# A graph network on one Trainium2 core: the begin of an edge pass, the read of its words and the evict of its sort moved

## The reference

```
h = x @ Wn + bn                                   # block 0, four layers of attention
for l in range(4):
    Q, K, V = h @ WQ[l] + bQ[l], h @ WK[l] + bK[l], h @ WV[l] + bV[l]
    scores = sum(Q[dst] * K[src]) * scale
    attn = softmax of scores over the edges of one dst
    h = layernorm(h + segment_sum(attn * V[src], dst) @ WO[l] + bO[l])
x = x + h @ Wout + bout
# block 1: attention of 8 heads with two types of edges
# block 2: weighted mean of the neighbours, concatenated, @ W
# block 3: segment_sum(norm * x[col], row) @ W.T + b
```

## Time and profile before

| | us |
|---|---|
| median of 3 runs | 7103.49 (7101.05 to 7110.28) |
| the profiled execution's own time | 7094.96 |
| its span | 7093.5 |
| mean granted TensorE clock, share of full | 0.811 |
| busy: PE, DVE | 4693.2 (66%), 4300.3 (61%) |
| busy: ACT, POOL | 2623.5 (37%), 4669.2 (66%) |
| POOL's gathers of the four passes (L1973), busy, idle before them | 2307.4, 887.5 |
| the weighing of their rows (L2141), busy | 729.4 |
| DVE's masks of dense units (L2254), busy, idle before them | 289.2, 413.0 |

### The profile page before, as it was taken

The page is one execution under the profiler, slowest core; times in us unless marked ns, Lnnn a source line. Parts: engine busy times, 40 slices in busy tenths (PEclk is TensorE's granted clock), DMA queues, the critical chain, the costliest instruction groups (busy, mean ns, idle before and its releaser), DMA issues. The chain is left out here.

```text
span 7093.5 us, 128253 instructions
## 1 busy us (share of the span) xinstructions
PE 4693.2 (66%) x28386; PEld 3840.8 (54%) x28387; DVE 4300.3 (61%) x13524; ACT 2623.5 (37%) x7476; POOL 4669.2 (66%) x4886
## 2 busy tenths in 40 slices
PE   5420377775777775777667777445555555998999
PEld 4310266654565554665546655323333334997998
DVE  7550266663666654666556666447776765776665
ACT  0200244434444443444444443315555543554111
POOL 1367577774777765777667777337777755776777
PEclk9555688887888887888778888677777776998999
DMA  5310233332333313333233333123333324333332
GB/s 188 99 37 0 62 92 91 88 84 63 87 90 89 89 50 96 89 90 89 62 86 89 89 90 82 49 89 105 105 105 105 105 69 117 97 96 84 96 95 82
DMA packets 404728, 615.56 MB, mean 87 GB/s; under 512 B 213510, under 2 KB 256049, under 8 KB 403940
## 3 DMA queue, kind: packets, MB, share of 16 engines
q0 software_dynamic: 169952, 363.29, 19.0%
q1 hardware_dynamic: 211190, 200.20, 9.9%
q10 hardware_dynamic: 23122, 47.29, 2.0%
HBM read 528.33 MB, written 82.09 MB: 86 GB/s over the span
## 5 line engine op out<-in xcount | busy, mean ns | idle before, releaser
L1973 POOL DMA_INDIRECT rows<-table_d,meta x2432 | 2307.4, 949 | 887.5 <-issue 728.6
L2037 PE MATMUL ps_total<-weighted_rows,ident 128*128 128x129 f32 (+1 forms) x6464 | 1404.3, 374 | 596.8 <-ACT weighted_rows L2197 483.7
L2037 PEld LDWEIGHTS ps_total<-weighted_rows,ident 128*128 128x128 f32 x6464 | 1149.8, 226 | 857.0 <-issue 670.4
L2373 DVE SCALAR_TENSOR_TENSOR prod<-rows,q_rows 128x129 f32<-128x129 f32 x2432 | 690.0, 293 | 639.3 <-issue 391.1
L1973 POOL DMA_INDIRECT rows<-pairs_d,meta x800 | 773.7, 967 | 257.7 <-issue 243.4
L2073 PE MATMUL dense_sums<-x_rows,dense_power_t 128*128 128x129 f32 x3528 | 593.9, 320 | 460.8 <-DVE dense_rows L2264 443.2
L2073 PEld LDWEIGHTS dense_sums<-x_rows,dense_power_t 128*128 128x128 f32 x3528 | 534.0, 230 | 501.5 <-issue 501.5
L2141 ACT ACTIVATE weighted_rows<-rows,power 128x129 f32<-128x129 f32 x2432 | 729.4, 389 | 5.1
L2159 ACT COPY dense_power_t<-dense_turned 128x512 f32<-128x512 f32 x504 | 265.1, 526 | 1030.7 <-PE dense_turned L2064 1022.1
L2197 ACT ACTIVATE weighted_rows<-once_weighted,of_relation 128x136 f32<-128x136 f32 x1600 | 485.6, 393 | 193.6 <-DVE once_weighted L2433 190.3
L2254 DVE CUSTOM_DVE_ANT_0 dense_masked<-dense_scores,dense_masked,dense_least 128x896 f32<-128x896 f32 x252 | 289.2, 1148 | 413.0 <-PE dense_scores L2055 289.9
(11 more groups left out here) (704 smaller groups left out, 8908.3 us busy)
## 6 DMA issues: line engine op xcount, KB each, us to landing
dense_masked<-dense_masks_d SPq DMA_DIRECT2D x252, 448.0 KB
rows<-table_d,meta POOLq DMA_INDIRECT x2432, 2.5
dense_masks_d<-unmasked ACTq DMA_DIRECT2D x9, 3136.0 KB
src_store<-near_window_d SPq DMA_DIRECT2D x50, 384.0 KB, 3.8
near_window<-near_window_d SPq DMA_DIRECT2D x48, 384.0 KB, 3.6
rows<-pairs_d,meta POOLq DMA_INDIRECT x800, 2.8
tile_rows<-table_d,tile_halves POOLq DMA_INDIRECT x441, 2.6
tile_rows<-made_d,tile_halves POOLq DMA_INDIRECT x441, 2.6
```

Of the source, the lines that this page charges most:

```text
L1973: pool.indirect_dma_start(rows[q][:, j, 0:width], None, table_d, bass.IndirectOffsetOnAxis(meta[q][:, j, number:number + 1], 0)).then_inc( ...
L2037: mm = pe.matmul(total[:, q, ds(part, 1), 0:W].rearrange("p a w -> p (a w)"), k.ident[:], wide[:, j % WS, :], start=False, stop=True, skip ...
L2373: own(dve.scalar_tensor_tensor(prod[:, j % 2, :], rows[q][:, j, :], -1.0, query, ALU.mult, ALU.mult, accum_out=score[:, j, :]))
```

## The change

1. *Begin.* The constants are no longer in a block of their own, so the engines don't meet behind them. ACT waits until the first group's list has landed, then issues x as 8 and 41 tiles. `fetch_layer` goes to SP, behind all its turns. PE turns the first two groups of x, turns the queries, scores the first unit, and then turns the other 11 groups, through two other banks; ACT copies the first two groups, the queries, then the other 11.
2. *Words.* PE reads a group's words for q=0 behind the first unit of a part (units 0 and 4), before behind units 2 and 6, and so raises `read[0]` there. The wait for `sum_taken` and the clearing of the sum stay with the adding of the columns.
3. *Sort.* The wait for `placed` and `scattered` and the evict move from step 5, behind the twelfth column of q=0 (j=11), to the head of step 0, behind the second column (j=1). `placed` is no longer waited for in step 2.

```
-        with nc.Block() as block:
-            @block.vector
-            def _(dve):
...
+        constants_of_pass(nc.vector)
...
                     turns(sp, body)
+                    if fetch is not None:
+                        fetch_layer(sp, m, k, *fetch)
...
                         pe.sem_inc(read[q], 1)
-
+                        return loaded
+
+                    def clear_sums(i, q):
                         pe.wait_ge(m["sum_taken"], i * 2 + (q + 1))
                         clear(q)
-                        return loaded
 
                     def add_columns(i, q, loaded, columns):
+                        if columns[0] == 0:
+                            clear_sums(i, q)
...
                                 if u in (0, 4):
                                     count_earlier(i)
+                                    loaded = load_words(i, 0)
                                 if u == 2:
-                                    add_columns(i, 0, load_words(i, 0), range(S))
+                                    add_columns(i, 0, loaded, range(S))
                                 if u == UNITS - 1:
-                                    loaded = load_words(i, 0)
                                     add_columns(i, 0, loaded, range(S // 2))
...
-                        for n in range(XGROUPS):
-                            if n == 0 or n == 6:
-                                pe.wait_ge(m[f"x_loaded{n // 6}"], 16)
-                            if n >= 2:
-                                pe.wait_ge(m["xt"], n - 1)
+                        def turn_x(n):
...
+                        pe.wait_ge(m["x_loaded0"], 16)
+                        turn_x(0)
+                        turn_x(1)
+                        pe.wait_ge(m["xt"], 2)
                         turn_queries(0)
                         scores(0, 0)
+                        pe.wait_ge(m["x_loaded1"], 16)
+                        for n in range(2, XGROUPS):
+                            pe.wait_ge(m["xt"], n - 1)
+                            turn_x(n)
+                        pe.wait_ge(m["xt"], XGROUPS)
                     turns(pe, body)
...
-                        for h, (t0, t1) in enumerate(((0, 24), (24, T))):
+                        act.wait_ge(listed[0], 48)
+                        for h, (t0, t1) in enumerate(((0, XFIRST), (XFIRST, T))):
...
-                    if fetch is not None:
-                        fetch_layer(act, m, k, *fetch)
...
                         if step == 0:
+                            dve.wait_ge(m["placed"], i + 1)
+                            dve.wait_ge(m["scattered"], i * 16 + 16)
+                            own(dve.tensor_copy(so.stretch[:], placed_ps))
+                            own(dve.scalar_tensor_tensor(so.idx[:], so.base[:], float(REGION - SW), so.start[:], ALU.min, ALU.add))
+                            own(dve.tensor_tensor(so.most[:], so.most[:], count_ps, ALU.max))
+                            own.wait()
+                            own(dve.scalar_tensor_tensor(so.base[:], count_ps, so.base[:], so.floor[:, ds(turn, 1)], ALU.add, ALU.max))
+                            dve.sem_inc(m["evicted"], 1)
...
                         if step == 2:
                             own.wait()
-                            dve.wait_ge(m["placed"], i + 1)
...
                         if step == 5:
...
-                            dve.wait_ge(m["scattered"], i * 16 + 16)
-                            own(dve.tensor_copy(so.stretch[:], placed_ps))
...
+XFIRST = 8
```

More of the change, by code:

```diff
@@ L1864, in edge_pass, with x_ps @@
             loaded_masks = [m["mask0"], m["mask1"]]
+            def x_ps(n):
+                return dense_ps[:, n] if n < 2 else (sum_ps, power_ps)[n % 2]
             masks_of = k.masks_d[0:DSPARE].rearrange("(t p c) r -> t p (c r)", p=P, c=NPAD)
@@ L1895, in step_of, with constants_of_pass @@
             return (loaded[j // PAIRS] >> ((6 if j < PAIRS else 0) + 2 * (j % PAIRS))) & 3
-        with nc.Block() as block:
-            @block.vector
-            def _(dve):
[L1900 to L1911, removed]
-                for q in range(2):
[L1913 to L1916, removed]
+        def constants_of_pass(dve):
+            if mode == "heads":
+                for r in range(2):
+                    dve.memset(relation[:, r:r + 1], float(1 - r))
+            if mode == "attend":
+                for q in range(2):
+                    dve.memset(rows[q][:, :, P:P + 1], 1.0)
+                dve.memset(k.x1[:, :, P:P + 1], 1.0)
+                dve.memset(least[:, 0:1], BIG)
+            if sort is not None:
+                dve.tensor_scalar(tile_no, k.iota_t[:], 1.0, None, ALU.add)
+                dve.tensor_copy(slot_no, so.slot_no[:])
+                dve.tensor_copy(keep, so.keep[:].rearrange("p t c -> p (t c)"))
+            for q in range(2):
+                dve.memset(resets[q][:, 0:1], HALF)
+                dve.memset(resets[q][:, S + 1:S + 2], HALF)
+                dve.memset(neg[q][:, :, S + 1:S + 2], HALF)
+            dve.memset(neg[0][:, :, 0:1], HALF)
+        constants_of_pass(nc.vector)
         with nc.Fori(0, epochs) as e:
@@ L2318, in sort_step @@
                             own(dve.tensor_tensor(at[:], before_ps.unsqueeze(2).to_broadcast([P, T, SC]), seen[:], ALU.add))
-                            dve.wait_ge(m["scattered"], i * 16 + 16)
-                            own(dve.tensor_copy(so.stretch[:], placed_ps))
-                            own(dve.scalar_tensor_tensor(so.idx[:], so.base[:], float(REGION - SW), so.start[:], ALU.min, ALU.add))
-                            own(dve.tensor_tensor(so.most[:], so.most[:], count_ps, ALU.max))
-                            own.wait()
-                            own(dve.scalar_tensor_tensor(so.base[:], count_ps, so.base[:], so.floor[:, ds(turn, 1)], ALU.add, ALU.max))
-                            dve.sem_inc(m["evicted"], 1)
                         if step == 6:
@@ L2698, in group_tiles, with fetch_layer @@
     return range(g * GB, min(g * GB + GB, T))
-def fetch_layer(act, m, k, I, l, last):
+def fetch_layer(sp, m, k, I, l, last):
     def matrix(n, j):
@@ L2707, in column @@
         return I[f"L0_gnn_{n}"][ds(j, 1)].rearrange("a (p n) -> (a p) n", n=1)
-    act.dma_start(k.raw["WV"][:], matrix("WV", l)).then_inc(m["fetched"], 16)
-    act.dma_start(k.raw["WO"][:], matrix("WO", l)).then_inc(m["fetched"], 16)
-    act.dma_start(k.bv[:], column("bV", l), allow_slow_non_contiguous=True).then_inc(m["fetched"], 16)
+    sp.dma_start(k.raw["WV"][:], matrix("WV", l)).then_inc(m["fetched"], 16)
+    sp.dma_start(k.raw["WO"][:], matrix("WO", l)).then_inc(m["fetched"], 16)
+    sp.dma_start(k.bv[:], column("bV", l), allow_slow_non_contiguous=True).then_inc(m["fetched"], 16)
     for n, o in (("ln_g", k.gb), ("ln_b", k.bb)):
-        act.dma_start(o[:], I[f"L0_gnn_{n}"][ds(l, 1)].rearrange("a n -> (a n)").partition_broadcast(P)).then_inc(m["fetched"], 16)
+        sp.dma_start(o[:], I[f"L0_gnn_{n}"][ds(l, 1)].rearrange("a n -> (a n)").partition_broadcast(P)).then_inc(m["fetched"], 16)
     if last:
-        act.dma_start(k.w1[:], I["L0_gnn_Wout"]).then_inc(m["fetched"], 16)
-        act.dma_start(k.b1[:], row(I["L0_gnn_bout"])).then_inc(m["fetched"], 16)
+        sp.dma_start(k.w1[:], I["L0_gnn_Wout"]).then_inc(m["fetched"], 16)
+        sp.dma_start(k.b1[:], row(I["L0_gnn_bout"])).then_inc(m["fetched"], 16)
         return
-    act.dma_start(k.raw["WQ"][:], matrix("WQ", l + 1)).then_inc(m["fetched"], 16)
-    act.dma_start(k.raw["WK"][:], matrix("WK", l + 1)).then_inc(m["fetched"], 16)
-    act.dma_start(k.bq[:], column("bQ", l + 1), allow_slow_non_contiguous=True).then_inc(m["fetched"], 16)
-    act.dma_start(k.bk[:], column("bK", l + 1), allow_slow_non_contiguous=True).then_inc(m["fetched"], 16)
+    sp.dma_start(k.raw["WQ"][:], matrix("WQ", l + 1)).then_inc(m["fetched"], 16)
+    sp.dma_start(k.raw["WK"][:], matrix("WK", l + 1)).then_inc(m["fetched"], 16)
+    sp.dma_start(k.bq[:], column("bQ", l + 1), allow_slow_non_contiguous=True).then_inc(m["fetched"], 16)
+    sp.dma_start(k.bk[:], column("bK", l + 1), allow_slow_non_contiguous=True).then_inc(m["fetched"], 16)
 def layer_turn(nc, k, I, l, last):
```

8 lines of the change are left out of this document (4 added, 4 removed).

## The result

The changed kernel takes **6993.68 us** (median of 4, 6990.34 to 6995.27) beside 7103.39 of the kernel before (median of 4, 7101.05 to 7110.28): ratio 0.9844, 95% interval 0.983 to 0.9858, or 110 us less. The forecast was 7021 with a range of 6978 to 7056. Direction and range hold; the gain is a third larger than the forecast 82.

A forecast was written before the change was run, and what follows sets the result against it. POOL's row gathers were taken to bound the middle of a pass. Begin 10.3, loop 5.4 and end 4.6 make 20.3 us a pass, 81 over four, plus 1 for the "heads" pass: 7103.5-82=7021 us, range 6978 to 7056.

The forecast's parts named there:

- Begin, 10.3 us a pass: Start of a pass: second dense unit at 818.6 in place of 828.91, 10.3 us won; bounds 7.4 and 15.7.
- Evict, 0.6 us a pair: Loop: the evict, moved ahead of PE's first score, costs DVE's chain 0.6 us per pair of turns.
- Lists, 10.8 us in the loop: Loop: lists 11.7 us earlier end DVE's 10.8 us of row waits; less nine pairs at 0.6, 5.4 us won.
- Words, "0": Loop: PE's two 302 ns reads move to after the first unit; 0.6 us shifts within a turn, net 0.
- The end, 4.6: End of a pass: POOL no longer late, last group starts behind the weighing; 4.6 us won, bounds 4.6 and 4.9.
- x late: Rival, begin: x bounds and lands at 815.3, so the begin wins only 4.0 us; 7047 us, chance 0.15.
- Lists late: Rival, loop: masks' waits in SP's in-order queue keep lists late, loop gains nothing; 7043 us, chance 0.10.
- POOL the only bound: Rival, loop: DVE keeps up, all 22.4 us of POOL's list waits count; 6954 us, chance 0.05.
- The wait for `placed`: Rival, loop: DVE's step 0 waits 5.0 us for PE's placing in each of 36 pairs; 7201 us, chance 0.05.
- The rule of the Trainium skill: Begin: moving DMAs to another engine saves only sequencer time, usually small; if so, near 7047 us.

The follow-up runs named there:

- evict_mixed: Changed kernel with the evict at the twelfth column in part 0 only; 10208 us, ratio 1.0242, on the slow chip.
- loads_doubled: Changed kernel plus two reads of a constant word on PE at the old place; 10538 us, ratio 1.0569, on the slow chip.
- no_evict: Changed kernel with the evict back at the twelfth column; 6989.84 us, ratio 0.9839, on the first chip.

## Why the prediction was right, and where it fell short

- **Begin, 10.3 us a pass: right in sum, in part by luck.** 9.7 in the trace; by itself, 42 us for four passes, where 10.3x4 is 41. But the 10.3 were worked out for the second dense unit of the first pass, and there the list took 8.3 us, not 5.1 (gathers from 793.87 and not 790.9), the last x landed at 810.7, not 809.0, and the unit came 7.6 us earlier (821.33), not 10.3. The first weighings of the four passes come 7.6, 12.2, 11.6 and 7.1 us earlier; the prediction had read no row of the middle two. By itself the new begin gives 7.0 in the begin and 3.1 in the loop. Which of its parts (no block, x behind the list and split 8 and 41, the weights on SP, the first scores ahead) gives how much was not separated.
- **Evict, 0.6 us a pair: right in size and place, wrong in what it is worth.** In the whole change it costs the loop 3.8 us a pass, 0.5 a pair, but most of that is given back at the begin and the end. By itself it costs 9 us, 0.25 a pair.
- **Lists, 10.8 us in the loop before the evict is taken off: right in mechanism, too large.** DVE's waits for rows went from 10.8 to none, and the release at the old place brings 10.2 back; but that lengthens the loop by 6.1 us a pass and the end by 3.7, 39 us in the whole time. The prediction took a wait that goes for time that is won.
- **Words, "0": the step that failed.** The prediction weighed the two reads of 302 ns as work that PE sheds in one place and takes up in another. It did not ask what else PE's sequencer had to do there: the register work for the 16 columns, which in the old place started only behind the reads. With lists at 6.1, the begin's 3.1 and the evict's 3.8 taken off, 7.4 of the loop's 12.8 us a pass are left for it, 30 us in all; the remainder by the totals is 33. That the total came within the range owes something to these errors' being of either sign.
- **The end, 4.6: near in size (5.4), wrong in the reason.** POOL is late there as before, only less. In the first pass the weighing ends at 1545.35+4.80=1550.15 and the gather that needs it starts at 1552.88, 2.7 us later and straight behind POOL's own work, where it was 4.9; forecast was 0.3. The mean of the four passes is 2.3 us, before 5.1, so 2.8 us a pass are won so. The rest of the 5.4 holds the ninth pair's share of the loop's gain, 12.8/8=1.6; the other 1.0 was not traced.

```profile
1545.35 4.80 ACT L2153 ACTIVATE weighted_rows<-rows,power 128x129 f32<-128x129 f32 x16
```

```profile
1552.88 0.94 POOL L1979 DMA_INDIRECT rows<-table_d,meta  x1 [0.30 <-issue]
```

- **Rivals.** x late: it landed 1.7 us later than forecast, not 6.3. Lists late: no, 9.3 us earlier. POOL the only bound: no, it now waits 7.8 us for weighed rows, and DVE's circle with PE stands. The wait for `placed`: DVE is never idle before any of the 72 evicts in the trace of the changed kernel. The rule of the Trainium skill, "DMA: Bandwidth & Descriptors", section "Issuing engines are not separate DMA queues", is neither borne out nor refuted for the weights' loads: the hold of some 15 us on ACT is real, but no run shows that it costs the pass anything.

## What to carry to other kernels

An engine's sequencer has work of its own, here two reads of a word and then 0.37 us of register work for each column, and it can do that ahead, while the engine still works at what it was given. Two reads of 0.3 us right ahead of such a run of columns took that lead away and cost up to 1.6 us, not 0.6; two whose word nobody used brought back 1.3 of it. So, where matmuls have addresses computed from data, read the data at a place where the sequencer's lead isn't needed next. Raising the semaphore that lets the next list be loaded at that earlier place is a second, separate gain. And a gain by removing one wait must be read against the next wait in line: the evict's move took away 8.5 us of waiting for the scatter in a pass's first turn, and 9.5 us more of waiting for the list stood behind. Likewise DVE's 10.8 us of waits for rows went, and the loop won 6.1.

## What the runs showed of the hardware

**PE's adding had a pace that isn't PE's.** In the kernel before, 16 columns took 5.91 us, 0.37 a column, nearly the same at every place (5.91 to 6.09 over 36), with a granted clock of 0.65 or of 0.91 in the mean. That is the pace of the sequencer's register work, which has the same 0.36 to 0.37 us a column in both kernels. In the changed kernel, where the sequencer has a lead of 1.7 us, the adding takes 4.31 to 5.67 us by the clock: 0.45 us for two columns at the upper of its two levels, 0.86 at the lower. So a faster clock gave nothing before, and does now.

**One chip was 40% slower, and there the change's parts did not pay.** On it the kernel before took 9971, 9979 and 9959 us in three sets; every kernel tried there holds the early read of the words and all or most of the new begin, and all are slower than the kernel before, by 2.4% (evict_mixed) to 5.7% (loads_doubled). The changed kernel itself was not run there. POOL and ACT are busy as long as on the first chip (4652.9 and 2624.3 us in evict_mixed). PE is busy for longer, 5294.5 us in evict_mixed and 4635.3 in no_evict on the first chip, with a mean granted clock of 0.716 and 0.814; but above all there are pauses of 5 to 20 us in which an engine does nothing and waits for nothing that the profile knows. One on ACT, from its timeline in evict_mixed:

```profile
1186.10 0.47 ACT L2171 COPY dense_power_t<-dense_turned 128x384 f32<-128x384 f32 x1
1206.25 0.58 ACT L2171 COPY dense_power_t<-dense_turned 128x512 f32<-128x512 f32 x1 [19.68 <-remote]
```

("remote" is a releaser that the profile couldn't find.) The only packet on any DMA queue between 1205 and 1206 was one of instructions:

```profile
DMA packets 1, 0.01 MB, mean 8 GB/s; under 512 B 0, under 2 KB 0, under 8 KB 0
...
q14 instruction: 1, 0.01, 3.2%
```

ACT goes on right behind it, as if it had waited for its own code. But the other pauses don't bear that out: of the 366 idle stretches of over 5 us on PE, DVE and ACT within that trace's four passes that no known releaser ends, only 7 end within 1 us behind such a packet, and 234 have no such packet within them; and there are as many of these packets in the passes (280) as in the changed kernel on the first chip (285). What the pauses are and why that chip differs from the other two stays open. So the 110 us are what the change gives on chips with 7100 us for the kernel before; a ratio holds for chips like the one it was measured on.
